# H's parts turned by TensorE instead of by DMA, spare transposes in two waits, and the last output tile stored in halves

## The chip, the core and the metric

One core of a Trainium2 chip runs the whole program as a single launch. The metric is the device time of one execution in microseconds (us). Three runs of the kernel before gave 870.17, 871.32 and 871.70 us, median 871.32.

## The reference, cut to what matters

```python
x = x + tanh(g_xattn[0]) * xattn(layernorm(x), ctx_4096, scales and zero points)
x = x + tanh(g_ffn[0]) * ffn(layernorm(x), w_gate, w_up, w_down, ri_in, ri_mid)

def ffn(x2):                       # 1024 rows, H = 1024, I = 2752, SELECT = 128
    A, g = quant_act(x2, ri_in)    # blocks of 16 in fp8, last 128 columns twice
    gate = A @ quant_w(w_gate).T * g          # int4 blocks of 16
    up = A @ quant_w(w_up).T * g
    h = silu(gate) * up
    Am, gm = quant_act(h, ri_mid)  # gm needs the maximum of |h| over ALL rows
    return Am @ quant_w(w_down).T * gm
```

`xattn` is a product of two tensors that are rounded to 8 bits. `quant_act` scales by one number from the maximum over the whole matrix, then rounds every block of 16 columns to fp8 with a scale of its own; the last 128 columns are rounded, and what is left over is rounded again.

## The kernel before, in words

The 1024 rows are eight tiles of 128 (t = 0 to 7). There are three stages. The first loads x and ctx, multiplies them, normalises and quantises (to about 200 us). The second multiplies the quantised rows by w_gate and w_up, tile by tile and 256 columns at a time, and writes h to DRAM (`multiply`, L1214 to L1220, to 615 us). The third waits for the maximum of |h| (`spread_max`, L1281), quantises h tile by tile, transposes it and multiplies it by w_down (`down`, L1270 to L1275). Every engine has its instructions in an order that is written out by hand; semaphores tie them together.

Numbers are kept to more than 16 bits by splitting each into a high and a low half in 16 bits: a block product is three matmuls (high x high, high x low, low x high). TensorE wants the column index of h on the partitions, so each tile must be turned. `H_CUTS` (L31) cuts the 22 blocks of 128 columns of each tile into parts: six for tile 0, four for tile 1, two halves for each later one. `H_PARTS` numbers them from 0. For one part the steps are:

- VectorE prepares it: `start_part` (L1753, two instructions), then `end_part` (L1762), which waits for ScalarE's `floor_magic` (L1081, L1085) and makes three sweeps (L1767, L1768, L1769). In the last part of a tile `quantise_twice` (L1447) follows for the outliers. It then signals `am_ready`.
- For the first `PE_PARTS` = 2 parts TensorE turns the part in 32 bits into a bank `tb` (`turn_h` L1264, `turn_piece` L1163, L1169), ScalarE copies the high half out (`hi_part` L876, L879) and VectorE subtracts it for the low half (`lo_part` L1408, L1411). The result lies in `amT`.
- For all others ScalarE and VectorE make the halves unturned in `nat_h` (L1104, L1785), and SP turns them by DMA: `turn_part` (L610, L615) with one transposition each for the high and the low half in tiles 0 and 1, `turn_half` (L617, L622) with one for both from tile 2 on.

VectorE's order is the loop at L1798: start of part n, then the low half of part n - 1 (`lo_h`, L1777), then the end of part n. From tile 2 on, the low half of the last part of the tile ahead comes before the start, and `finish` (L1788, L1794), which adds the product to x, stands in its place. TensorE's order is the loop at L1283:

```python
for hf in range(2):
    last = down(t % 2, hf, range(ks.start, ks.stop))
    if ks.stop == DK:
        last.then_inc(y_done, 1)
    if hf == 0 and n + 1 < PE_PARTS:
        turn_h(n + 1)
```

`hf` are the two halves of 512 output columns. ScalarE's order is: high half of part n, then `floor_magic` of part n + 1 (L1087 to L1106). SP's list is that of L630 to L650: the transpositions of tiles 0 and 1, each tile's followed by the load of the tile two on (`load_tile` L536); then for each later tile the store of an output tile (`store_out` L625, L628), a transposition, a load of x, the other transposition, a load.

Of the kernel before, what the change touches and what calls it, by code (L numbers as in the profile page):

```python
# [9 lines left out]
F16 = mybir.dt.float16  # L10
# [5 lines left out]
P = 128  # L16
# [5 lines left out]
NT = ROWS // P  # L22
# [5 lines left out]
MW = 512  # L28
DK = -(-I // P)
DH = DK // 2  # L30
H_CUTS = ((0, 3, 7, 11, 15, 19, DK), (0, 5, DH, 16, DK)) + ((0, DH, DK),) * (NT - 2)  # L31
H_PARTS = [(t, slice(a, b)) for t, cuts in enumerate(H_CUTS) for a, b in zip(cuts, cuts[1:])]
PE_PARTS = 2
HALVES = sum(1 for t, ks in H_PARTS if t < 2)
H_SMALL = 1e-20
HPAD = DK * P
# [28 lines left out]
def gated_block(nc, x, ctx_in, g_xattn, g_ffn, s1, z1, s2, z2, w_gate, w_up, w_down, ri_in, ri_mid, out):  # L65
    x_d = x.rearrange("b l h -> (b l) h").rearrange("(t p) h -> t p h", p=P)
    out_d = out.rearrange("b l h -> (b l) h").rearrange("(t p) h -> t p h", p=P)
    ctx_d = ctx_in.rearrange("b s h -> (b s) h").rearrange("(t p) h -> t p h", p=P)

    with ExitStack() as ctx:  # L70
# [3 lines left out]
        def sem(name):  # L74
            return ctx.enter_context(nc.semaphore(name))
# [25 lines left out]
        a_lo = mid[:, 4096:8192].bitcast(F16).rearrange("p (k r) -> p k r", k=KT)  # L101
        a_both = mid[:, 0:8192].bitcast(F16).rearrange("p (q r) -> p q r", q=2 * KT)
        ring = mid[:, 8192:16384].bitcast(F16).rearrange("p (s v k n) -> p s v k n", s=2, v=2, k=KT)
        amT = mid[:, 0:2 * DK * P].bitcast(F16).rearrange("p (s g v k r) -> p s g v k r", s=2, g=2, v=2, k=DH)
        o = 2 * DK * P
        mgh = mid[:, o:o + DH * P]
        o += DH * P
# [17 lines left out]
        o += 4 * H  # L125
        ro_a = big[:, o:o + 4 * SELECT].rearrange("p (s n) -> p s n", s=4)
        p_ring = big[:, 0:KT * 2 * PW].bitcast(F16).rearrange("p (v k n) -> p v k n", v=2, k=KT)
        nat_h = wbuf[:, :, :].rearrange("p b h -> p (b h)")[:, 0:HPAD].bitcast(F16).rearrange("p (g v n) -> p g v n", g=2, v=2)
        silu = sb("silu", [P, 2, UW], F32)
        h_out = sb("h_out", [P, 2, UW], F32)  # L130
        a_nat = [x[:, :, :].rearrange("p s n -> p (s n)").bitcast(BF16) for x in (silu, h_out)]
# [3 lines left out]
        ident = sb("ident", [P, P], F32)  # L135
# [156 lines left out]
        def part_of(t, k):  # L292

            return next(n for n, (at, ks) in enumerate(H_PARTS) if at == t and ks.start <= k < ks.stop)

        def parts_in(t, g):

            return [n for n, (at, ks) in enumerate(H_PARTS) if at == t and ks.start // DH == g]

        def nat_part(v, ks):  # L300

            g = ks.start // DH
            return nat_h[:, g, v, (ks.start - g * DH) * P:(ks.stop - g * DH) * P]

        def turned_part(i, v, ks):

            g = ks.start // DH
            return amT[:, i, g, v, ks.start - g * DH:ks.stop - g * DH, :]

        def loads_before(b, u):  # L310

# [6 lines left out]
        def buf(n):  # L318

            return (n + 1) % 4  # L320
# [5 lines left out]
        def _(sp):  # L326
# [283 lines left out]
            def turn_part(n):  # L610

                t, ks = H_PARTS[n]
                sp.wait_ge(nat_h_lo, n - PE_PARTS + 1)
                for v in range(2):
                    sp.dma_start_transpose(turned_part(t, v, ks), nat_part(v, ks)).then_inc(part_turned[n], 16)  # L615

            def turn_half(t, i, g):  # L617

                if g == 0:
                    sp.wait_ge(y_done, 2 * (t - 1))  # L620
                sp.wait_ge(nat_h_lo, part_of(t, g * DH) - PE_PARTS + 1)
                sp.dma_start_transpose(amT[:, i, g, :, :, :].rearrange("p v k r -> p (v k) r"),  # L622
                                       nat_h[:, g, :, :].rearrange("p v n -> p (v n)")).then_inc(h_turned[g], 16)

            def store_out(t, i):  # L625

                sp.wait_ge(y_out, t + 1)
                sp.dma_start(out_d[t], x1_t[:, i, :]).then_inc(out_stored[i], 16)  # L628

            for n in range(PE_PARTS, HALVES):  # L630
                turn_part(n)
                t, ks = H_PARTS[n]
                if ks.stop == DK:

                    sp.wait_ge(turned, PE_PARTS)
                    load_tile(t + 2, t)
            for t in range(2, NT):
                i = t % 2
                store_out(t - 2, i)
# [4 lines left out]
                turn_half(t, i, 1)  # L644
                if t + 2 < NT:
                    load_tile(t + 2, i)
            for t in (NT - 2, NT - 1):
                store_out(t, t % 2)
            for i in range(2):
                sp.wait_ge(out_stored[i], 16 * (NT // 2))  # L650
            sp.wait_ge(x1_gone, 16 * X1_FIRST)
            sp.wait_ge(x1_stored, 16 * (NT - X1_FIRST))

# [144 lines left out]
        def _(act):  # L798
# [289 lines left out]
            for n, (t, ks) in enumerate(H_PARTS):  # L1088
                if n < PE_PARTS:
                    hi_part(n, n % 4, turned_part(t, 0, ks), ks.stop - ks.start, P)  # L1090
                else:
                    if n == PE_PARTS:

                        act.wait_ge(nat_lo, UNITS_D * UNIT_PIECES + PIECE_LOOP)
                    act.wait_ge(am_ready, n + 1)
                    g = ks.start // DH
                    if t in (1, 2) and ks.start == g * DH:

                        for m in parts_in(t - 1, g):
                            if m >= PE_PARTS:  # L1100
                                act.wait_ge(part_turned[m], 32)
                    elif t > 2:
                        act.wait_ge(h_turned[g], 16 * (t - 2))
                    act.activation(nat_part(0, ks), h_in[:, t % 2, ks.start * P:ks.stop * P], ACT.Copy).then_inc(nat_h_hi, 1)  # L1104
                if n + 1 < len(H_PARTS):
                    floor_magic(n + 1, H_PARTS[n + 1][1])  # L1106
# [3 lines left out]
        def _(pe):  # L1110
            pe.wait_ge(consts_made, 2)
            def spread_max(column, out):

                return pe.transpose(out, column.to_broadcast([P, P]), ident[:])

            def turn_x(t):

# [116 lines left out]

            for n in range(P_PIECES):
                pe.wait_ge(piece_turned[buf(n)], 16)
            for m in OPENING[0:2]:
                multiply_open(m)
            for j in range(4):
# [30 lines left out]
            def down(i, hf, ks):  # L1270
                for k in ks:
                    for left, right in ((0, wd_hi), (0, wd_lo), (1, wd_hi)):
                        last = pe.matmul(acc[2 * i + hf][:], amT[:, i, k // DH, left, k % DH, :], right[:, k, hf * MW:(hf + 1) * MW],  # L1273
                                         start=(k == 0 and left == 0 and right is wd_hi), stop=(k == DK - 1 and left == 1))
                return last  # L1275


            for b in range(3):
                pe.wait_ge(piece_turned[b], turns_before(b, UNITS_D) * 16)
            pe.wait_ge(part_max, 2)  # L1280
            spread_max(gmx[:, 1:2], tb[3][:, 0:P]).then_inc(all_max, 1)  # L1281
            turn_h(0)
            for n, (t, ks) in enumerate(H_PARTS):  # L1283
                if n < PE_PARTS:

                    pe.wait_ge(lo_done, n + 1)
                elif t < 2:
                    pe.wait_ge(part_turned[n], 32)
# [14 lines left out]
        def _(dve):  # L1303
# [484 lines left out]
            def finish(t, i):  # L1788

                dve.wait_ge(x1_loaded[i], 16 * (t // 2 + 1))  # L1790
                for hf in range(2):
                    dve.wait_ge(y_done, 2 * t + (hf + 1))
                    xs = x1_t[:, i, hf * MW:(hf + 1) * MW]
                    last = dve.scalar_tensor_tensor(out=xs, in0=acc[2 * i + hf][:], scalar=gs[:, 5:6], in1=xs,  # L1794
                                                    op0=ALU.mult, op1=ALU.add)
                last.then_inc(y_out, 1)

            for n, (t, ks) in enumerate(H_PARTS):  # L1798
                i = t % 2
# [48 lines left out]
```

## Time and profile before

| what | value |
|---|---|
| median of three runs | 871.32 us |
| the profiled execution's own time | 870.89 us |
| its span in the trace | 869.0 us |
| TensorE matmul, busy | 738.5 us, 85% |
| VectorE, busy | 617.9 us, 71% |
| GpSimd, busy | 356.6 us, 41% |
| ScalarE, busy | 305.8 us, 35% |
| TensorE's share of the chain that ended last | 73% |
| VectorE's share of that chain | 19% |
| mean granted TensorE clock | 0.947 |

The span is the part of the execution that the profiler's instructions cover. The chain follows the last instruction back to what released each step. Matmuls are pipelined and their ends are modelled, so in a row with a count the time from the first start to the next start says more than a mean. A granted clock of 1.00 is 2.4 GHz and 0.50 is 1.2 GHz.

### The profile page before, as it was taken

To read this page: it belongs to the slowest core of one execution; us is meant where nothing else is said; L and a number is where in the kernel's file an instruction comes from. 1 tells how busy PE (TensorE), PEld (TensorE's weight loads), DVE (VectorE), ACT (ScalarE), POOL (GpSimd) and SP (SyncE) were. 2 spreads that over 40 slices of the span, in tenths; PEclk is the share of its full clock that TensorE was granted. 3 is DMA by queue.
4 is the path that set the end of the run, shared out by engine and by line. 5 is a ranking of instruction groups with operands and counts; after the bars stand their busy time and mean duration, and the time that the engine had idled before them with its cause. 6 is when DMAs were issued, how large, how long until landed. Compare 5 with 4: busy or idle time off the path is not lost.

```text
span 869.0 us, 10408 instructions
## 1 busy us (share of the span) xinstructions
PE 738.5 (85%) x3478; PEld 336.5 (39%) x3483; DVE 617.9 (71%) x1006; ACT 305.8 (35%) x370; POOL 356.6 (41%) x194
## 2 busy tenths in 40 slices
PE   1488300399999999999999999999698799999998
PEld 0234100154544444444444444444243344444443
DVE  5789999999265656565757676732699999989710
ACT  3657595333133434344434343520122122211100
POOL 4992789523156666666657585820000000000000
PEclk9998755599999999999999999999799999999999
DMA  8810757733449796979797979843224665663420
GB/s 315 312 50 34 209 173 190 170 64 80 75 95 210 162 220 159 222 163 232 162 220 168 228 165 220 185 104 116 98 42 118 164 158 151 174 151 101 101 58 24
DMA packets 228355, 131.36 MB, mean 151 GB/s; under 512 B 201312, under 2 KB 212576, under 8 KB 227296
## 3 DMA queue, kind: packets, MB, share of 16 engines
q1 hardware_dynamic: 228320, 130.92, 61.8%
q8 instruction: 18, 0.29, 0.1%
q14 instruction: 17, 0.14, 0.0%
HBM read 61.88 MB, written 19.66 MB: 94 GB/s over the span
## 4 chain that ended last, share of the span: by engine, by line
PE 73%; DVE 19%; POOL 4%; DMA 2%; issue 1%; ACT 1%; SPq 0%; DVEq 0%; ACTq 0%
PE acc L1218 48%; PE acc L1273 24%; POOL big L688 2%; DVE big L1484 2%; DVE tb L1393 1%; DVE big L1488 1%; PE acc L1154 1%; DVE big L1366 1%; DVE bst L1315 1%; DVE big L1468 1%; DVE tb L1473 1%; DMA mid<-wbuf 1%; DVE h_in L1417 1%; POOL mid L690 1%; DMA big<-in_x_dram 1%
## 5 line engine op out<-in xcount | busy, mean ns | idle before, releaser
L1218 PE MATMUL acc<-mid 128*128 128x512 f16 x1920 | 415.2, 379 | 0.8 <-DVE h_out L1505 0.8
L1218 PEld LDWEIGHTS acc<-mid 128*128 128x128 f16 x1920 | 187.7, 98 | 227.2 <-DVE h_out L1505 1.2
L1273 PE MATMUL acc<-big,mid 128*128 128x512 f16 x1056 | 232.1, 383 | 9.7 <-DMA mid<-wbuf 8.6
L779 POOL TENSOR_TENSOR h_in<-wbuf,h_in 128x1024 f16<-128x1024 f32 (+1 forms) x56 | 114.4, 2044 | 113.1 <-ACT h_in L1056 113.0
L1273 PEld LDWEIGHTS acc<-big,mid 128*128 128x128 f16 x1056 | 103.7, 99 | 137.5 <-issue 9.1
L696 POOL TENSOR_TENSOR wbuf<-wbuf,w_inv 128x1024 f32<-128x1024 f32 (+1 forms) x67 | 124.9, 1870 | 39.9 <-DVE w_inv L1399 39.9
L1505 DVE SCALAR_TENSOR_TENSOR h_out<-acc,gs,silu 128x256 f32<-128x256 f32 (+1 forms) x88 | 41.7, 474 | 121.7 <-ACT silu L908 95.7
L1393 DVE TENSOR_REDUCE tb<-wbuf 128x64 f32<-128x1024 f32 (+1 forms) x67 | 79.0, 1179 | 40.3 <-DMA wbuf<-in_L_ffn_w_gate_dram 21.5
L1056 ACT ACTIVATE h_in<-wbuf 128x1024 f16<-128x1024 f32 (+1 forms) x56 | 57.0, 1019 | 119.1 <-DVE wbuf L1405 119.1
L858 ACT ACTIVATE wbuf<-wbuf 128x1024 f32<-128x1024 f32 (+1 forms) x67 | 68.1, 1016 | 82.8 <-POOL wbuf L696 82.0
L1218 PE MATMUL acc<-big,mid 128*128 128x384 f16 x192 | 33.4, 336 | 48.1 <-DMA mid<-big 48.1
L908 ACT ACTIVATE silu<-acc,gs 128x256 f32<-128x256 f32 (+1 forms) x88 | 40.1, 455 | 76.2 <-PE acc L1218 73.3
L1405 DVE SCALAR_TENSOR_TENSOR wbuf<-wbuf,tb 128x1024 f32<-128x1024 f32 (+1 forms) x56 | 65.1, 1163 | 0.3 <-issue 0.2
L1104 ACT ACTIVATE wbuf<-h_in 128x1408 f16<-128x1408 f32 (+4 forms) x20 | 22.1, 1105 | 112.3 <-DVE h_in L1461 60.8
L1218 PEld LDWEIGHTS acc<-big,mid 128*128 128x128 f16 x192 | 19.2, 100 | 62.0 <-issue 50.1
L1794 DVE SCALAR_TENSOR_TENSOR mid<-acc,gs,mid 128x512 f32<-128x512 f32 x16 | 11.6, 745 | 40.9 <-PE acc L1273 40.9
L1085 ACT ACTIVATE mid<-mid,floor_bias 128x1408 f32<-128x1408 f32 (+7 forms) x22 | 24.8, 1128 | 44.4 <-DVE mid L1760 44.4
L1510 DVE TENSOR_REDUCE hm<-h_out 128x256 f32 (+2 forms) x88 | 34.0, 387 | 2.6
L714 POOL TENSOR_TENSOR big<-big 128x1024 f16<-128x1024 f32 x8 | 18.8, 2372 | 41.0 <-ACT big L903 41.0
L688 POOL TENSOR_SCALAR big<-big 128x1024 f32<-128x1024 f32 x8 | 29.5, 3684 | 11.3 <-ACT big L814 10.7
L1154 PE MATMUL acc<-mid,big 128*128 128x512 bf16 x125 | 32.7, 418 | 0.2
L1399 DVE RECIPROCAL w_inv<-tb 128x64 f32<-128x64 f32 (+1 forms) x56 | 30.2, 539 | 2.1 <-DVE tb L1396 0.2
(161 smaller groups left out, 616.4 us busy)
## 6 DMA issues: line engine op xcount, KB each, us to landing
h_in<-h_d SPq DMA_DIRECT2D x8, 1376.0 KB, 7.0
wbuf<-in_L_ffn_w_gate_dram SPq DMA_DIRECT2D x21, 512.0 KB, 4.2
wbuf<-in_L_ffn_w_up_dram SPq DMA_DIRECT2D x21, 512.0 KB, 4.1
h_d<-h_out SPq DMA_DIRECT2D x80, 128.0 KB, 3.4
big<-in_ctx_dram SPq DMA_DIRECT2D x16, 512.0 KB, 7.0
wbuf<-in_L_ffn_w_down_dram SPq DMA_DIRECT2D x16, 512.0 KB, 4.5
big<-in_x_dram SPq DMA_DIRECT2D x8, 512.0 KB, 6.7
x_d<-big SPq DMA_DIRECT2D x8, 512.0 KB, 3.0
```

The costliest lines, as they stand in the source:

```text
L688: pool.tensor_scalar(w, w, 255.0, MAGIC, ALU.min, ALU.add).then_inc(ctx_round, 1)
L696: pool.tensor_tensor(w, w, spread(w_inv[0:rows, b, 0:cols // BLK]), ALU.mult).then_inc(w_scaled, 1)
L779: pool.tensor_tensor(nat[s % 4][:, H:H + cols], wbuf[:, s % 4, 0:cols], nat[s % 4][:, 0:cols], ALU.subtract)\
L858: act.activation(wbuf[0:rows, b, 0:cols], wbuf[0:rows, b, 0:cols], ACT.Copy, bias=MAGIC, scale=W_UP)\
L908: act.activation(silu[:, m % 2, 0:cols], acc[m % 4][:, 0:cols], ACT.Silu, scale=gs[:, 2:3]).then_inc(silu_done, 1)
L1056: act.activation(nat[s % 4][:, 0:cols], wbuf[:, s % 4, 0:cols], ACT.Copy).then_inc(nat_hi, 1)
L1154: pe.matmul(acc[pair(t) + hf][:], aT[:, k, t * P:(t + 1) * P], ctxq[:, b * KT + k, hf * MW:(hf + 1) * MW], start=(k == 0), stop=False)
L1218: last = pe.matmul(acc[m % 4][:, 0:cols], left[:, k, s * P:(s + 1) * P], w[:, right, k, 0:cols], start=(k == 0 and left is a_hi and right ...
L1273: last = pe.matmul(acc[2 * i + hf][:], amT[:, i, k // DH, left, k % DH, :], right[:, k, hf * MW:(hf + 1) * MW], start=(k == 0 and left == ...
L1393: dve.tensor_reduce(top, blocks(wbuf[0:rows, b, 0:cols]), AX_X, ALU.max, apply_absolute_value=True).then_inc(scale_step, 1)
L1405: dve.scalar_tensor_tensor(out=w, in0=w, scalar=MAGIC, in1=spread(block_scale(b, looped)[0:rows, 0:cols // BLK]), op0=ALU.subtract, op1=AL ...
L1505: dve.scalar_tensor_tensor(out=h_out[:, m % 2, 0:cols], in0=acc[m % 4][:, cols:2 * cols], scalar=gs[:, 2:3], in1=silu[:, m % 2, 0:cols], o ...
```

## The change

Five edits. (1) `PE_PARTS` becomes 7: all six parts of tile 0 and the first of tile 1 are turned by TensorE. (2) Tile 1's first cut is at block 4, not 5. (3) The high and low half of a part lie side by side in `nat_h` and in `amT`, and one transposition turns both; SP loads tile 2 once TensorE has turned tile 0. (4) TensorE transposes the identity into a bank that nobody reads: 14 times (`WARM`) in the wait ahead of the gate and up products, and 6 and 22 times around the maximum of |h|. (5) The last output tile is finished and stored in two halves.

```diff
-H_CUTS = ((0, 3, 7, 11, 15, 19, DK), (0, 5, DH, 16, DK)) + ((0, DH, DK),) * (NT - 2)
+H_CUTS = ((0, 3, 7, 11, 15, 19, DK), (0, 4, DH, 16, DK)) + ((0, DH, DK),) * (NT - 2)
-PE_PARTS = 2
+PE_PARTS = 7
+WARM = 14
+FIRST_PARTS = sum(1 for t, ks in H_PARTS if t == 0)
...
+        def part_at(v, ks):
+            first = 2 * (ks.start // DH) * DH + 2 * (ks.start % DH) + v * (ks.stop - ks.start)
+            return first, first + (ks.stop - ks.start)
...
+        def nat_both(ks):
+            return nat_h[:, part_at(0, ks)[0] * P:part_at(1, ks)[1] * P]
+        def turned_both(i, ks):
+            return amT[:, i, part_at(0, ks)[0]:part_at(1, ks)[1], :]
...
                 sp.wait_ge(nat_h_lo, n - PE_PARTS + 1)
-                for v in range(2):
-                    sp.dma_start_transpose(turned_part(t, v, ks), nat_part(v, ks)).then_inc(part_turned[n], 16)
+                sp.dma_start_transpose(turned_both(t, ks), nat_both(ks)).then_inc(part_turned[n], 16)
...
+            sp.wait_ge(turned, FIRST_PARTS)
+            load_tile(2, 0)
             for n in range(PE_PARTS, HALVES):
                 turn_part(n)
-                t, ks = H_PARTS[n]
-                if ks.stop == DK:
-                    sp.wait_ge(turned, PE_PARTS)
-                    load_tile(t + 2, t)
+            sp.wait_ge(turned, PE_PARTS)
+            load_tile(3, 1)
...
-            for t in (NT - 2, NT - 1):
-                store_out(t, t % 2)
+            store_out(NT - 2, 0)
+            for hf in range(2):
+                sp.wait_ge(y_out, NT + hf)
+                sp.dma_start(out_d[NT - 1][:, hf * MW:(hf + 1) * MW], x1_t[:, 1, hf * MW:(hf + 1) * MW]).then_inc(out_half[hf], 16)
...
+            def keep_busy(n, bank):
+                for _ in range(n):
+                    pe.transpose(tb[bank][:, 0:P], ident[:], ident[:])
...
             for n in range(P_PIECES):
                 pe.wait_ge(piece_turned[buf(n)], 16)
+            pe.wait_ge(nat_a_lo, 1)
+            for i in range(WARM):
+                pe.transpose(acc[3][:, 0:P], ident[:], ident[:])
...
+            keep_busy(6, 2)
             pe.wait_ge(part_max, 2)
             spread_max(gmx[:, 1:2], tb[3][:, 0:P]).then_inc(all_max, 1)
+            keep_busy(22, 2)
             turn_h(0)
...
-                last.then_inc(y_out, 1)
+                    if hf == 1 or t == NT - 1:
+                        last.then_inc(y_out, 1)
```

Three places of the instruction order, before and after. First TensorE's list from the maximum of |h| on, before (`gmx` is the maximum, `tb` the bank a transpose writes, `acc` the product):

```order
L1114 MATMUL tb<-ident,gmx 128x128
L1169 MATMUL tb<-ident,h_in 128x128 x3
L1273 MATMUL acc<-big,mid 128x512 x9
L1169 MATMUL tb<-ident,h_in 128x128 x4
L1273 MATMUL acc<-big,mid 128x512 x1047
```

and in the changed kernel:

```order
L1137 MATMUL tb<-ident 128x128 x6
L1132 MATMUL tb<-ident,gmx 128x128
L1137 MATMUL tb<-ident 128x128 x22
L1192 MATMUL tb<-ident,h_in 128x128 x3
L1300 MATMUL acc<-big,mid 128x512 x9
L1192 MATMUL tb<-ident,h_in 128x128 x4
L1300 MATMUL acc<-big,mid 128x512 x21
L1192 MATMUL tb<-ident,h_in 128x128 x4
L1300 MATMUL acc<-big,mid 128x512 x24
L1192 MATMUL tb<-ident,h_in 128x128 x4
L1300 MATMUL acc<-big,mid 128x512 x24
```

The transposes of part m + 1 now stand between the two output halves of part m up to part 6; 28 spare ones stand around the maximum. Second, ScalarE's list for parts 1 to 3 (L1085 is `floor_magic`), before:

```order
L879 ACTIVATE mid<-tb 128x512
L1085 ACTIVATE mid<-mid,floor_bias 128x512
L1104 ACTIVATE wbuf<-h_in 128x512
L1085 ACTIVATE mid<-mid,floor_bias 128x512
L1104 ACTIVATE wbuf<-h_in 128x512
L1085 ACTIVATE mid<-mid,floor_bias 128x512
```

and in the changed kernel (L897 is the copy out of `tb`, L1103 `floor_magic`):

```order
L897 ACTIVATE mid<-tb 128x512
L1103 ACTIVATE mid<-mid,floor_bias 128x512
L897 ACTIVATE mid<-tb 128x512
L1103 ACTIVATE mid<-mid,floor_bias 128x512
L897 ACTIVATE mid<-tb 128x512
L1103 ACTIVATE mid<-mid,floor_bias 128x512
```

The high halves of parts 2 to 6 are now copied out of the bank that TensorE writes, not out of `h_in`; the places in the list are the same. Third, SP's list in tiles 0 and 1, before:

```order
L615 DMA_TRANSPOSE mid<-wbuf 128x4x128 x6
L615 DMA_TRANSPOSE mid<-wbuf 128x3x128 x2
L537 ISA
L537 DMA h_in<-h_d 128x2752
L615 DMA_TRANSPOSE mid<-wbuf 128x5x128 x2
L615 DMA_TRANSPOSE mid<-wbuf 128x6x128 x2
L615 DMA_TRANSPOSE mid<-wbuf 128x5x128 x2
L615 DMA_TRANSPOSE mid<-wbuf 128x6x128 x2
```

and in the changed kernel:

```order
L553 DMA h_in<-h_d 128x2752
L630 DMA_TRANSPOSE mid<-wbuf 128x14x128
L630 DMA_TRANSPOSE mid<-wbuf 128x10x128
L630 DMA_TRANSPOSE mid<-wbuf 128x12x128
L553 ISA
L553 DMA h_in<-h_d 128x2752
```

Sixteen transpositions became three, of 14, 10 and 12 blocks, and the load of tile 2 comes before them.

## Rows read from the trace of the kernel before

**Rows 1.** The page, its groups of instructions: the gate and up products.
```profile
L1218 PE MATMUL acc<-mid 128*128 128x512 f16 x1920 | 415.2, 379 | 0.8 <-DVE h_out L1505 0.8
```

**Rows 2.** The chain that ended last: start (us), length, engine, work.
```profile
200.55 414.65 PE acc L1218 x1944
...
659.19 27.87 PE acc L1273 x129
687.07 5.15 DMA mid<-wbuf
692.35 172.80 PE acc L1273 x792
```

**Rows 3.** Timeline of the opening: start, length, engine, line, work, idle time before.
```profile
160.12 4.20 POOL L714 TENSOR_TENSOR big<-big 128x1024 f16<-128x1024 f32 x2
...
166.91 9.54 PE L1218 MATMUL acc<-big,mid 128*128 128x384 f16 x48 [48.06 <-DMA mid<-big]
```

**Rows 4.** Timeline of the start of the down product, and the first matmuls of tile 2.
```profile
622.15 0.90 PE L1169 MATMUL tb<-ident,h_in 128*128 128x128 f32 x3 [4.79 <-DVE h_in L1769]
...
624.23 3.74 PE L1273 MATMUL acc<-big,mid 128*128 128x512 f16 x9 [1.18 <-DVE mid L1411]
...
627.80 0.60 PE L1169 MATMUL tb<-ident,h_in 128*128 128x128 f32 x4
...
628.24 7.29 PE L1273 MATMUL acc<-big,mid 128*128 128x512 f16 x33
628.44 0.60 ACT L879 ACTIVATE mid<-tb 128x512 f16<-128x512 f32 x1 [4.25 <-PE tb L1169]
...
629.07 0.69 DVE L1411 TENSOR_TENSOR mid<-tb,mid 128x512 f16<-128x512 f32 x1 [1.58 <-ACT mid L879]
...
659.19 2.98 PE L1273 MATMUL acc<-big,mid 128*128 128x512 f16 x13 [2.26 <-DMA mid<-wbuf]
...
692.35 19.98 PE L1273 MATMUL acc<-big,mid 128*128 128x512 f16 x84 [4.49 <-DMA mid<-wbuf]
```

**Rows 5.** Timeline of VectorE in tile 0: sweeps of parts 3 to 5, outlier steps.
```profile
635.18 0.69 DVE L1769 TENSOR_TENSOR h_in<-h_in,mid 128x512 f32<-128x512 f32 x1
...
639.24 0.69 DVE L1769 TENSOR_TENSOR h_in<-h_in,mid 128x512 f32<-128x512 f32 x1
...
641.70 0.49 DVE L1767 SCALAR_TENSOR_TENSOR h_in<-mid,h_in 128x320 f32<-128x320 f32 x1
...
646.40 0.29 DVE L1461 TENSOR_TENSOR h_in<-h_in,ro_h 128x128 f32<-128x128 f32 x1
```

**Rows 6.** VectorE's low part in tile 1; landing of SP's transpositions of L622.
```profile
653.58 0.82 DVE L1785 TENSOR_TENSOR wbuf<-h_in,wbuf 128x640 f16<-128x640 f32 x1
...
DMA to landing us min/median/max: 5.1/5.2/6.9
```

**Rows 7.** Windows and a burst: PE, PEld, DVE, ACT, POOL busy; granted clock; DMA; GB/s.
```profile
71.00:71.50 0.50, 0.13 (x2) 0.14 (x3) 0.50 (x5) 0.46 (x1) 0.00 (x0) 0.67 0.00 0
...
77.50:78.00 0.50, 0.50 (x3) 0.18 (x2) 0.47 (x1) 0.50 (x1) 0.00 (x0) 0.50 0.00 0
...
73.30 1.04 PE L1122 MATMUL tb<-identb,h_out 128*128 128x128 bf16 x8 [0.90 <-DVE h_out L1359]
...
617.00:617.50 0.50, 0.29 (x1) 0.13 (x1) 0.29 (x2) 0.00 (x0) 0.00 (x0) 0.80 0.56 197
...
657.00:658.00 1.00, 0.00 (x0) 0.00 (x0) 1.00 (x2) 0.35 (x1) 0.00 (x0) 1.00 1.17 215
...
692.00:692.50 0.50, 0.15 (x1) 0.13 (x2) 0.43 (x3) 0.00 (x0) 0.00 (x0) 0.90 0.64 229
...
695.50:696.00 0.50, 0.50 (x3) 0.17 (x2) 0.50 (x1) 0.50 (x1) 0.00 (x0) 0.69 0.00 0
```

**Rows 8.** The end: SP's last store, and the window in which its bytes move.
```profile
865.95 0.34 SPq L628 DMA_DIRECT2D out_dram<-mid  x1
...
867.00:868.00 1.00, 0.00 (x0) 0.00 (x0) 0.00 (x0) 0.00 (x0) 0.00 (x0) 1.00 1.01 410
```

More of the change, by code:

```diff
@@ L103, in gated_block @@
         ring = mid[:, 8192:16384].bitcast(F16).rearrange("p (s v k n) -> p s v k n", s=2, v=2, k=KT)
-        amT = mid[:, 0:2 * DK * P].bitcast(F16).rearrange("p (s g v k r) -> p s g v k r", s=2, g=2, v=2, k=DH)
+        amT = mid[:, 0:2 * DK * P].bitcast(F16).rearrange("p (s k r) -> p s k r", s=2, r=P)
         o = 2 * DK * P
@@ L127, in gated_block @@
         p_ring = big[:, 0:KT * 2 * PW].bitcast(F16).rearrange("p (v k n) -> p v k n", v=2, k=KT)
-        nat_h = wbuf[:, :, :].rearrange("p b h -> p (b h)")[:, 0:HPAD].bitcast(F16).rearrange("p (g v n) -> p g v n", g=2, v=2)
+        nat_h = wbuf[:, :, :].rearrange("p b h -> p (b h)")[:, 0:HPAD].bitcast(F16)
         silu = sb("silu", [P, 2, UW], F32)
@@ L260, in gated_block @@
         y_out = sem("y_out")
+        out_half = [sem(f"out_half{i}") for i in range(2)]
         out_stored = [sem(f"out_stored{i}") for i in range(2)]
@@ L298, in parts_in @@
             return [n for n, (at, ks) in enumerate(H_PARTS) if at == t and ks.start // DH == g]
+        def part_at(v, ks):
+            first = 2 * (ks.start // DH) * DH + 2 * (ks.start % DH) + v * (ks.stop - ks.start)
+            return first, first + (ks.stop - ks.start)
         def nat_part(v, ks):
-            g = ks.start // DH
-            return nat_h[:, g, v, (ks.start - g * DH) * P:(ks.stop - g * DH) * P]
+            a, b = part_at(v, ks)
+            return nat_h[:, a * P:b * P]
         def turned_part(i, v, ks):
-            g = ks.start // DH
-            return amT[:, i, g, v, ks.start - g * DH:ks.stop - g * DH, :]
+            a, b = part_at(v, ks)
+            return amT[:, i, a:b, :]
+        def nat_both(ks):
+            return nat_h[:, part_at(0, ks)[0] * P:part_at(1, ks)[1] * P]
+        def turned_both(i, ks):
+            return amT[:, i, part_at(0, ks)[0]:part_at(1, ks)[1], :]
         def loads_before(b, u):
@@ L621, in turn_half @@
                 sp.wait_ge(nat_h_lo, part_of(t, g * DH) - PE_PARTS + 1)
-                sp.dma_start_transpose(amT[:, i, g, :, :, :].rearrange("p v k r -> p (v k) r"),
-                                       nat_h[:, g, :, :].rearrange("p v n -> p (v n)")).then_inc(h_turned[g], 16)
+                ks = H_PARTS[part_of(t, g * DH)][1]
+                sp.dma_start_transpose(turned_both(i, ks), nat_both(ks)).then_inc(h_turned[g], 16)
             def store_out(t, i):
@@ L646, in _ @@
                     load_tile(t + 2, i)
-            for t in (NT - 2, NT - 1):
-                store_out(t, t % 2)
+            store_out(NT - 2, 0)
+            for hf in range(2):
+                sp.wait_ge(y_out, NT + hf)
+                sp.dma_start(out_d[NT - 1][:, hf * MW:(hf + 1) * MW], x1_t[:, 1, hf * MW:(hf + 1) * MW]).then_inc(out_half[hf], 16)
             for i in range(2):
-                sp.wait_ge(out_stored[i], 16 * (NT // 2))
+                sp.wait_ge(out_stored[i], 16 * (NT // 2 - i))
+                sp.wait_ge(out_half[i], 16)
             sp.wait_ge(x1_gone, 16 * X1_FIRST)
@@ L1100, in _ @@
                             if m >= PE_PARTS:
-                                act.wait_ge(part_turned[m], 32)
+                                act.wait_ge(part_turned[m], 16)
                     elif t > 2:
@@ L1270, in down @@
             def down(i, hf, ks):
+                hi, lo = (turned_part(i, v, ks) for v in range(2))
                 for k in ks:
-                    for left, right in ((0, wd_hi), (0, wd_lo), (1, wd_hi)):
-                        last = pe.matmul(acc[2 * i + hf][:], amT[:, i, k // DH, left, k % DH, :], right[:, k, hf * MW:(hf + 1) * MW],
-                                         start=(k == 0 and left == 0 and right is wd_hi), stop=(k == DK - 1 and left == 1))
+                    for left, right in ((hi, wd_hi), (hi, wd_lo), (lo, wd_hi)):
+                        last = pe.matmul(acc[2 * i + hf][:], left[:, k - ks.start, :], right[:, k, hf * MW:(hf + 1) * MW],
+                                         start=(k == 0 and left is hi and right is wd_hi), stop=(k == DK - 1 and left is lo))
                 return last
@@ L1287, in _ @@
                 elif t < 2:
-                    pe.wait_ge(part_turned[n], 32)
+                    pe.wait_ge(part_turned[n], 16)
                 else:
```

## The prediction

> **What bounds the kernel now.** I read the page first, then the chain that ended last, then the stretches around the two places where TensorE stands idle, and last the granted clock in short windows. The page's group of the gate and up products shows 1920 matmuls with only 0.8 us of idle time ahead of them, and that wait is for VectorE (h_out, L1505) [rows 1]. In the chain, TensorE takes over at 200.55 us and runs without a wait to 615.20. The second stage (the down product) begins behind that: 129 matmuls from 659.19 to 687.06, a transposition that is issued at 687.07, and 792 matmuls from 692.35 to 865.15 [rows 2]. So before 200 us and between 615 and 692 us VectorE and the transpositions decide; elsewhere TensorE does, at 27.87 / 129 = 0.216 us for a matmul. What the change is worth is what it does to the moment 692.35, to the speed just behind it, and to the last store.
>
> **The opening (14 transposes of the identity).** TensorE waits there until 166.91 us; the first of the two rows of POOL's residual work is half over at 162.2, which is what releases the new transposes [rows 3]. At half clock one costs 0.21 us (three take 0.90 us with their latency, and at full clock four start and end within 0.44 us before the next matmul begins, 0.11 each [rows 4]), so 14 end near 165.2, 1.7 us before they could delay anything. If they bring the clock up, the first ten or so matmuls (384 columns, 0.32 us in place of 0.16) give back 1.7 us. I cost this at **nothing**: VectorE releases TensorE at 200.55 [rows 1, 2], and its own work ahead of that does not wait for TensorE. The 0.8 us wait grows to 2.5 us. If that cover were gone, the gain would be 1.7 us at most.
>
> **Tile 0 of H by TensorE.** Four more parts of tile 0 and the first part of tile 1 (four blocks, was five by DMA) now go as the first two did: TensorE turns part m+1 between the two output halves of part m, ScalarE copies the high part out of PSUM, VectorE makes the low part. I follow three clocks. TensorE for a part of four blocks: 12 matmuls (2.59), four transposes (0.44), 12 matmuls (2.59), together **5.62 us**. VectorE's own work for one: the ends of its last sweep lie 4.05 us apart now (635.18 to 639.24) [rows 5]. But VectorE makes the low part m+1 *before* it may do the three sweeps of part m+2, and that low part now needs the transposes, which stand behind 12 matmuls. From the start of part m on TensorE it is 2.59 + 0.60 (transposes to their last end) + 0.04 + 0.61 (ScalarE) + 0.03 + 0.69 (VectorE) [rows 4] = 4.56 us until the low part m+1 is made. So TensorE is always fed and VectorE is held to TensorE's pace of 5.62 us, not its own 4.05.
>
> With the clock up: part 0 is ready at 622.10; its three transposes, 0.90 us now [rows 4], take 0.5, so the first matmul is at 623.85, 0.4 earlier; 9 matmuls to 625.8; part 1 is ready at 626.0, its transposes take 626.05 to 626.49, the second half ends at 628.43. There part 1 starts; part 3 starts two cycles on, at 628.43 + 2 x 5.62 = 639.67, and the low part 4 is made at 639.67 + 4.56 = 644.23. The sweeps of part 5, which now begin at 641.70, thus begin at 644.26: **2.6 us late**; the outlier steps behind them [rows 5] move to 645.8 to 649.2. In tile 1 TensorE must finish 12 + 9 matmuls between the transposes of part 5 (649.25) and those of part 6 (654.11), and ScalarE's step for the seven-block part comes behind that copy, some 0.2 us more for VectorE; the low part of seven blocks in place of six adds 0.1 to 0.2. From there on VectorE's list is the old one. The transposition of tile 2's first half is issued at 687.07 + 2.9 and lands as long after it as now (5.3 us [rows 2]): **695.25 instead of 692.35, +2.9 us**. Bounds: +2.0 (nothing added in tile 1, 0.5 saved in handing over) and +4.3, below.
>
> **Tile 1's own wait.** TensorE is through part 6 (24 matmuls) at 661.7. The seven-block part is swept at 660.1, its low part is made at 662.6, and one transposition of 14 blocks must land. The nearest rows: two of five blocks landed 4.8 us after the low part (653.58 + 0.82 to 659.19), 22 blocks take 5.2 [rows 4, 6]. I take 4.4, so 667.0: an idle time of 5.3 us where the old one was 2.3. Behind it 108 matmuls, 23.3 us, and 1.7 for eight of them at half clock, end at 692.0. That is before 695.25, so this wait costs nothing by itself; it is the cover of the single transposition and of the new cut too, which I cost at nothing. SP passes fewer transpositions (3 in place of 16) ahead of the third tile's load; the load of tile 2 moves up to about 649.7, off the path either way.
>
> **The clock behind 692.** In the trace the clock fell during idle times of 4.5 us (692.0 to 692.5), and of about 2 us (617.0 to 617.5 and 71.0 to 71.5), and stayed up across 2.3 us (657 to 658) [rows 7]. The new idle time ahead of tile 2 is 3.3 us. It lies between, and I take it to fall (three chances in four): the restart then loses about what it loses now: the clock is at half from 692.4 to 695.65 (0.90 and 0.69 of full speed in the two windows of half a microsecond [rows 7]), and 3.3 us at half clock are 1.65 us lost. I put down -0.2 for a shorter slow piece; ends 0 and -1.7.
>
> **The 28 transposes at 615 us** cost nothing in place: six take 0.64 us (1.3 at half clock) behind 615.2 and the maximum is wanted at 617.07; 22 take 2.4 us, or 4.7 at half clock, and end at 622.05 at the latest, before part 0 is ready.
>
> **The last tile in halves.** The last store is issued at 865.95; its 512 KB move at 410 GB/s [rows 8], 1.3 us. Half of it is **-0.6 us**; ends 0 and -0.9. The first half goes 7 us earlier, beside nothing.
>
> **Sum** against this execution's own 870.89 us (span 869.0): +2.9 - 0.2 - 0.6 = +2.1, 873.0. The median of the three runs, 871.32, is 0.43 above it, so **873.4** on its scale. About 0.2% (1.7 us) is what a measurement of this kernel can tell from no change.
>
> **Rivals.**
> *Cold start.* The spare transposes do not bring the clock up, or it is low again when the down product begins, since from 622.1 (at full clock from 619.7) to 623.85 TensorE does nothing but the three transposes of part 0. Evidence: it stood at half at 77.5 although 16 transposes and then matmuls had run from 71.4 on [rows 7]. Then nine matmuls take 3.7 us as now [rows 4], the transposes of part 1 come at 627.5, and everything behind them 1.4 us later: the low part 4 at 645.6, tile 2's half at 696.6 (+4.25), sum +4.25 - 0.4 - 0.6 = +3.2, **874.5**. By "TensorE: Matmul & The Clock Gate" of the Trainium skill, Part 4, the full clock does not engage for transposes, which would make this the certain case; the burst at 71 to 74 us agrees with it but had gaps, so the trace leaves it open.
> *Clock kept ahead of tile 2.* If the 3.3 us do not let it fall, the restart is 1.5 us quicker than in my sum: **871.9**. For it: 2.3 us kept it [rows 7].
> *Faster, the other sign: the hand-over does not pace VectorE.* This is so only if the low part m+1 is made before VectorE has finished preparing part m+2, that is within 4.05 us of the last one; I find 5.62. If it held, VectorE would lose none of the 2.6 us and save the 1.6 us for which it now stands idle ahead of its second low part (627.5 to 629.07 [rows 4]): 692.35 - 1.6 + 0.3, full clock behind it (-1.7), -0.6 for the store: 867.3, **867.7**. Against it stands the order of TensorE's list: the transposes are behind 12 matmuls.
>
> **How the numbers follow.** My forecast (clock up at 623.8, down at 695) 0.38; cold start 0.30; clock kept 0.14; not paced 0.10; other mishaps, of either sign, 0.08. Slower than 873.06: 0.65 of the forecast (0.25), nine tenths of the cold start (0.27), and 0.04 of the rest: 0.56. Faster than 869.58: the last rival and a few hundredths of the rest, 0.11. Within: 0.33. The range of 8 in 10 leaves out the unpaced case and the far end of the cold one: 870.9 to 875.3.
>
> **What would show it.** In the new trace: a wait of about 1 to 1.7 us of VectorE ahead of each low part of parts 2 to 4, released by ScalarE's copy out of tb; TensorE without a gap from 626 to 648; then an idle time near 5 us in tile 1 and near 3 us before tile 2, released by transpositions; the first matmul of tile 2 at 695.3 (696.6 if cold); TensorE's wait at 200 us grown to about 2.5. I am wrong if VectorE does not wait in tile 0, or if the moment of 692.35 does not move back.

## The result, and the profile after

| | before | changed |
|---|---|---|
| median | 870.75 us (4 runs) | 876.34 us (4 runs, 875.49 to 876.90) |
| ratio | 1 | 1.006, interval 1.004 to 1.008 |
| the profiled execution's own time | 870.89 us | 875.49 us |
| its span | 869.0 us | 873.5 us |

The change makes the kernel slower by 0.6%. The direction was forecast, the size was not: 873.4 was the forecast, 875.3 the upper end of the range.

The page's groups of the changed kernel, where L1241 is the gate and up product and L1300 the down product:

```profile
L1241 PE MATMUL acc<-mid 128*128 128x512 f16 x1920 | 415.2, 379 | 0.4 <-DVE h_out L1534 0.4
...
L1300 PE MATMUL acc<-big,mid 128*128 128x512 f16 x1056 | 235.8, 386 | 8.4 <-DMA mid<-wbuf 7.2
```

TensorE's wait for VectorE in the opening went from 0.8 us [rows 1] to 0.4. The waits of the down product for transpositions sum to 7.2 us, where the page of the kernel before has 8.6. So TensorE's idle time in these groups fell, and what is lost does not stand in this view.

The chain that ended last (start, length, engine, work), to be laid beside [rows 2]:

```profile
200.55 414.65 PE acc L1241 x1944
...
623.86 4.02 PE acc L1300 x9
...
664.93 4.35 DMA mid<-wbuf
669.32 22.73 PE acc L1300 x95
692.05 5.13 DMA mid<-wbuf
697.32 172.80 PE acc L1300 x792
870.15 0.75 DVE mid L1823
```

The long chain of gate and up products begins at 200.55 and lasts 414.65 us in both kernels, to the hundredth. So nothing ahead of 615.20 moved. The first matmul of tile 2 was at 692.35 and is at 697.32: **+4.97 us**. The 792 matmuls behind it take 172.80 us in both. From the end of VectorE's last instruction (870.90) to the end of the span it is 2.6 us, where it was 3.1. So +4.97 - 0.5 is the whole difference of the two spans, 4.5 us.

The timeline of tile 0 in the changed kernel, TensorE's transposes (L1192) and VectorE's low parts (L1440), which answers to [rows 4, 5]:

```profile
622.14 0.55 PE L1192 MATMUL tb<-ident,h_in 128*128 128x128 f32 x3 [2.44 <-DVE h_in L1798]
...
627.67 1.06 PE L1192 MATMUL tb<-ident,h_in 128*128 128x128 f32 x4
...
629.40 0.69 DVE L1440 TENSOR_TENSOR mid<-tb,mid 128x512 f16<-128x512 f32 x1 [2.14 <-ACT mid L897]
...
633.56 0.60 PE L1192 MATMUL tb<-ident,h_in 128*128 128x128 f32 x4
...
634.83 0.69 DVE L1440 TENSOR_TENSOR mid<-tb,mid 128x512 f16<-128x512 f32 x1 [1.55 <-ACT mid L897]
...
639.18 0.60 PE L1192 MATMUL tb<-ident,h_in 128*128 128x128 f32 x4
...
640.45 0.69 DVE L1440 TENSOR_TENSOR mid<-tb,mid 128x512 f16<-128x512 f32 x1 [1.74 <-ACT mid L897]
...
644.80 0.60 PE L1192 MATMUL tb<-ident,h_in 128*128 128x128 f32 x4
...
646.06 0.69 DVE L1440 TENSOR_TENSOR mid<-tb,mid 128x512 f16<-128x512 f32 x1 [1.72 <-ACT mid L897]
646.67 0.48 DVE L1796 SCALAR_TENSOR_TENSOR h_in<-mid,h_in 128x320 f32<-128x320 f32 x1
```

The sets of transposes are 5.6 to 5.9 us apart, and ahead of the low parts of parts 1 to 4 VectorE stands idle for 1.55 to 2.14 us until ScalarE's copy is there. The sweeps of part 5 begin at 646.67; they began at 641.70 [rows 5]. That is 4.97 us, the whole delay, and it is there before tile 1 begins.

Windows of the changed kernel (busy PE, PEld, DVE, ACT, POOL; granted clock; DMA; GB/s), beside [rows 7]:

```profile
164.00:165.00 1.00, 1.00 (x7) 1.00 (x6) 0.96 (x2) 0.00 (x0) 0.34 (x1) 0.50 1.15 212
165.00:165.50 0.50, 0.50 (x3) 0.21 (x1) 0.50 (x2) 0.00 (x0) 0.00 (x0) 0.67 1.15 214
165.50:166.00 0.50, 0.03 (x1) 0.00 (x0) 0.47 (x2) 0.00 (x0) 0.00 (x0) 1.00 1.09 184
...
622.50:623.00 0.50, 0.19 (x2) 0.00 (x0) 0.47 (x2) 0.28 (x1) 0.00 (x0) 0.71 0.00 0
...
629.00:629.50 0.50, 0.50 (x3) 0.23 (x2) 0.10 (x1) 0.50 (x2) 0.00 (x0) 0.50 0.00 0
629.50:630.00 0.50, 0.50 (x4) 0.23 (x3) 0.50 (x1) 0.48 (x1) 0.00 (x0) 0.96 0.00 0
...
697.00:698.00 1.00, 0.68 (x3) 0.32 (x4) 0.83 (x4) 0.00 (x0) 0.00 (x0) 0.90 0.66 242
698.00:699.00 1.00, 1.00 (x4) 0.33 (x3) 0.90 (x4) 0.00 (x0) 0.00 (x0) 0.50 0.59 234
```

The clock came up at 165.3 behind nothing but spare transposes, stayed up to 622.7, fell there and rose at 629.5. It was at half (1.2 GHz) for the nine matmuls of part 0's first output half, for the four transposes of part 1 and for the first two or so of the 21 matmuls behind them. It fell again in tile 1's wait, at 667.1, and, last, at 697.8, after the restart.

### The profile page after: what moved, and what is told of

The parts are those of the page before. It is cut to its first block, busy times and chain, and to the rows that moved or that the text cites. A ratio compares the mean times of both kernels' runs of the same rounds, so it can differ in the third digit from the quotient of the medians.

```text
span 873.5 us, 10523 instructions
## 1 busy us (share of the span) xinstructions
PE 745.4 (85%) x3544; PEld 343.9 (39%) x3544; DVE 618.2 (71%) x1006; ACT 305.8 (35%) x370; POOL 356.4 (41%) x194
## 4 chain that ended last, share of the span: by engine, by line
PE 74%; DVE 16%; POOL 3%; DMA 3%; ACT 1%; SPq 1%; issue 1%; DVEq 0%; ACTq 0%
PE acc L1241 47%; PE acc L1300 25%; DVE big L1513 2%; POOL big L706 2%; DVE big L1517 2%; PE acc L1177 1%; DVE tb L1422 1%; DMA mid<-wbuf 1%; DMA big<-in_ctx_dram 1%; DVE big L1497 1%; DVE big L1395 1%; DVE tb L1502 1%; DVE bst L1344 1%; POOL mid L708 1%; DMA wbuf<-in_L_ffn_w_gate_dram 1%
## 5 line engine op out<-in xcount | busy, mean ns | idle before, releaser
L1241 PE MATMUL acc<-mid 128*128 128x512 f16 x1920 | 415.2, 379 | 0.4 <-DVE h_out L1534 0.4
L1241 PEld LDWEIGHTS acc<-mid 128*128 128x128 f16 x1920 | 187.8, 98 | 226.7 <-DVE h_out L1534 0.9
L1300 PE MATMUL acc<-big,mid 128*128 128x512 f16 x1056 | 235.8, 386 | 8.4 <-DMA mid<-wbuf 7.2
L1300 PEld LDWEIGHTS acc<-big,mid 128*128 128x128 f16 x1056 | 104.7, 99 | 136.6 <-issue 10.4
L1122 ACT ACTIVATE wbuf<-h_in 128x1408 f16<-128x1408 f32 (+3 forms) x15 | 19.1, 1270 | 98.4 <-DVE h_in L1490 55.8
L1262 PE MATMUL acc<-ident 128*128 128x128 f32 x14 | 3.1, 417 | 45.4 <-POOL big L732 45.4
L1103 ACT ACTIVATE mid<-mid,floor_bias 128x1408 f32<-128x1408 f32 (+7 forms) x22 | 24.8, 1128 | 41.5 <-DVE mid L1789 41.5
L1241 PE MATMUL acc<-big,mid 128*128 128x384 f16 x192 | 32.0, 326 | 3.2 <-DMA mid<-big 3.2
L1177 PE MATMUL acc<-mid,big 128*128 128x512 bf16 x128 | 30.6, 395 | 0.0
```

The source lines that it names most:

```text
L1177: pe.matmul(acc[pair(t) + hf][:], aT[:, k, t * P:(t + 1) * P], ctxq[:, b * KT + k, hf * MW:(hf + 1) * MW], start=(k == 0), stop=False)
L1241: last = pe.matmul(acc[m % 4][:, 0:cols], left[:, k, s * P:(s + 1) * P], w[:, right, k, 0:cols], start=(k == 0 and left is a_hi and right ...
L1300: last = pe.matmul(acc[2 * i + hf][:], left[:, k - ks.start, :], right[:, k, hf * MW:(hf + 1) * MW], start=(k == 0 and left is hi and righ ...
```

## Experiments

All are edits of the changed kernel. Instruction lists that are identical over the gate and up products reached the end of the gate and up products between 614.1 and 617.1 us in the profiles of these kernels, so that single times scatter by some 3 us. I therefore read the third stage against its own start: E is the end of the long chain of gate and up products, R the first matmul of tile 2. "VectorE's wait" is its idle time ahead of the low parts, for ScalarE's copy out of `tb`, between 612 and 712 us. For the kernel before and for the changed one its lines are:

```profile
DVE mid L1411 <- ACT mid L879: 2.0, 2, 1.6
...
DVE mid L1440 <- ACT mid L897: 7.2, 4, 2.1
```

| kernel | VectorE's wait | R - E | 792 matmuls | ratio to before (interval) |
|---|---|---|---|---|
| before | 2.0 | 77.15 | 172.80 | 1 |
| changed | 7.2 | 82.12 | 172.80 | 1.006 (1.004 to 1.008) |
| e1_parts_back | 2.2 | 77.58 | 173.47 | 1.0006 (0.9992 to 1.0021) |
| e2_no_spare | 7.4 | 82.22 | 172.80 | 1.0052 (1.0034 to 1.007) |
| e3_clock_kept | 4.8 | 79.78 | 171.11 | 1.0012 (0.9996 to 1.0028) |
| e4_whole_store | 7.2 | 82.08 | 172.80 | 1.0055 (1.0034 to 1.0076) |
| e5_short_tile0 | 2.2 | 77.15 | 171.12 | 0.9978 (0.9965 to 0.999) |
| e6_two_kept | 0.3 | 75.64 | 172.69 | 0.9968 (0.9953 to 0.9984) |
| e7_no_warm | 7.3 | 82.06 | 172.80 | 1.0058 (1.0036 to 1.008) |
| e8_three_kept | 1.3 | 76.53 | 171.11 | 0.9966 (0.9947 to 0.9985) |
| e10_turn_ahead | 4.5 | 79.27 | 172.79 | 1.0022 (1.0006 to 1.0038) |
| e11_two_busy | 0.3 | 76.47 | 170.95 | 0.996 (0.9945 to 0.9975) |

R - E less VectorE's wait is 74.8 to 75.4 us in all of them but e11 (76.2), where spare transposes reach into the restart. So R - E follows VectorE's wait. The column of the 792 matmuls is a term of its own, the clock behind the restart: at 171.1 us it stayed up, at 172.8 us it was low for some 3 us.

### The parts back

```diff
-H_CUTS = (..., (0, 4, DH, 16, DK))    PE_PARTS = 7
+H_CUTS = (..., (0, 5, DH, 16, DK))    PE_PARTS = 2
```

SP's list is as before, with one transposition for each part.

> The changed kernel with the parts as before: two of them turned by TensorE, tile 1's first cut at block 5, SP's list in the old order; one transposition for both halves, the spare transposes and the last tile in halves stay. Pacing theory (VectorE is held to TensorE's pace in tile 0, and that is all of the loss): the sweeps of part 5 begin at about 641.7 us as before, the first matmul of tile 2 at 692.4, no wait of VectorE ahead of the low parts 2 to 5; with the store's 0.5 us the median is 870.2, 6 us under the changed kernel. Rival (the spare transposes cost, or the joined transpositions land late): at least 873, with the moment of 692.4 at 694 or later.

The wait of VectorE ahead of its low parts in this kernel (total, times, longest; E is 617.13):

```profile
DVE mid L1439 <- ACT mid L896: 2.2, 1, 2.2
```

Its chain:

```profile
202.48 414.65 PE acc L1240 x1944
...
694.71 173.47 PE acc L1299 x792
```

R - E is 77.58, 4.5 us less than in the changed kernel, and there is one wait, not four. The joined transpositions, the spare transposes and the halves, all still there, cost no more than 0.4 us together at this point. By the absolute marks this looks like the rival, whose price was 694 or later: R is at 694.71 and not at 692.4. But the long chain began 1.93 us late (202.48 in place of 200.55), ahead of everything that was edited, and only 0.4 us is left of the rest. The median was 872.58 beside 871.89 for the kernel before, not 1 us under it; the 0.5 us of the store did not show in the times. The parts, with the new cut and the order of SP's list that go with them, are the cause.

### The clock kept up

```diff
-            keep_busy(22, 2)
+            keep_busy(40, 2)
             turn_h(0)
+            keep_busy(10, 2)
```

> The changed kernel with 40 spare transposes in place of 22 behind the maximum and 10 more behind the transposes of part 0, so that TensorE idles for less than a microsecond before the first down matmul. Theory (the clock's fall at 622.7 is one term, the pacing the other): the clock stays up from 615 to 660, part 0's nine matmuls take 1.95 us and not 4.0, the sweeps of part 5 begin at 644.3 in place of 646.7, tile 2 starts 2.4 us earlier, near 694.9, and the time falls by 2.4 (by 0.7 to 1 if the clock is then found low for longer behind 695), to about 874. Rival (all of the loss is the clock): the time falls to 871 or less.

VectorE's wait in this kernel:

```profile
DVE mid L1441 <- ACT mid L897: 4.8, 4, 1.7
```

The chain of the same kernel:

```profile
199.43 414.65 PE acc L1241 x1944
...
693.86 171.11 PE acc L1300 x792
```

R - E is 693.86 - 614.08 = 79.78: the clock's share of the 4.97 us is 2.34, the pace's share is 2.63. The forecast case of the prediction gave +2.9 for the pace with the clock up. "All of the loss is the clock" falls. A part of the better time is a third thing: TensorE stood idle for 1.90 us ahead of tile 2, the clock stayed up, and the 792 matmuls took 171.11 us in place of 172.80.

### TensorE made faster than VectorE in tile 0

```diff
-            def down(i, hf, ks):
+            def down(i, hf, ks, short=False):
...
+                        if short and right is wd_lo:
+                            continue
...
-                    last = down(t % 2, hf, range(ks.start, ks.stop))
+                    last = down(t % 2, hf, range(ks.start, ks.stop), t == 0)
```

This leaves out w_down's low half in tile 0, 44 matmuls.

> The changed kernel without the high x low products of tile 0 (it leaves out 44 of the 132 matmuls of that tile, that is w_down's low half there). TensorE's cycle for a four-block part is then 16 x 0.216 + 0.44 = 3.9 us, less than VectorE's 4.05. Pacing theory: VectorE no longer waits ahead of the low parts 3 to 5, its sweeps of part 5 begin at 641 and not at 646.7, tile 2 starts at 691.5 to 692, and the time is about 870, though TensorE's own saving in tile 0 (9.5 us) comes before a wait for VectorE anyway. Rival (TensorE's work, not its pace over VectorE, is what counts): all 9.5 us are saved, 866.8. Rival (the loss comes from tile 1's new wait for its 14-block transposition): no change in where tile 2 starts, 697.

VectorE's wait in this kernel:

```profile
DVE mid L1442 <- ACT mid L897: 2.2, 4, 0.9
```

Its chain:

```profile
635.78 0.66 PE tb L1192 x4
...
639.91 0.67 PE tb L1192 x4
...
692.49 171.12 PE acc L1302 x792
```

TensorE's sets of transposes are now 4.13 us apart (635.78 to 639.91), close to VectorE's own 4.05, and VectorE's last two waits are 0.25 and 0.23 us. R - E is 77.15, the value of the kernel before to the hundredth, although seven parts still go by TensorE, the clock is still low at the start (from 623.2 to 630.0) and the new wait in tile 1 is still there (5.25 us). This settles that VectorE is held to TensorE's pace, and that tile 1's wait costs nothing. Of the 9.5 us of matmuls left out 5.0 came back at R.

### Two parts, then three, with the clock kept

```diff
-PE_PARTS = 7
+PE_PARTS = 2        (3 in e8_three_kept)
```

Both with the old cuts, with SP's list in the old order and with the spare transposes of e3_clock_kept.

> Two parts by TensorE and the old cuts, one transposition for both halves, the last tile in halves, and enough spare transposes (6, 40 and 10) that the clock stays up until the first down matmul. From the end of the gate and up products, theory: part 0's matmuls end 2 us earlier, VectorE's wait ahead of its second low part goes from 1.6 us to about 0.6, so the first matmul of tile 2 comes 490.3 us after the start of the long gate and up chain (491.8 before, 496.8 in the changed kernel, 494.4 with seven parts and the clock kept); with the store in halves the whole is 1.5 to 2 us under the kernel before. Rival (the spare transposes buy nothing without the parts): 491.8 and no more than 0.5 us under the kernel before.

VectorE's wait in this kernel:

```profile
DVE mid L1440 <- ACT mid L896: 0.3, 1, 0.3
```

Its chain:

```profile
168.94 448.16 PE acc L1240 x2112
...
692.74 172.69 PE acc L1299 x792
```

E is 168.94 + 448.16 = 617.10, R - E is 75.64, which puts R 490.3 us behind the start of the long chain (taken as E - 414.65), as forecast: 1.5 us less than before.

> As e6_two_kept, but with three parts by TensorE. If each part that TensorE turns beyond the second holds VectorE by the difference of the two paces, this one costs 0.8 us (the first such wait is shorter, since VectorE is then not yet ahead): the first matmul of tile 2 at 491.1 us after the start of the long chain. If the loss in the changed kernel comes from the seventh part and the new cut in tile 1 alone, it equals e6_two_kept.

VectorE's wait in this kernel:

```profile
DVE mid L1440 <- ACT mid L896: 1.3, 2, 1.1
```

Its chain:

```profile
200.19 414.65 PE acc L1240 x1944
...
691.37 171.11 PE acc L1299 x792
```

R - E is 76.53: the third part costs 0.89 us (forecast 0.8), and VectorE's wait grew by 1.0 us. One more part, one more wait; tile 1, which has the old cuts and goes by DMA in both kernels, has no share in it.

The restart, 171.11 in place of 172.69, does not speak for three parts. In e8_three_kept the clock fell in tile 1's wait, so that tile 1's 132 matmuls took 30.35 us, where they took 28.66 in e6_two_kept. That filled the wait ahead of tile 2 (2.71 us in place of 4.47), and there the clock then stayed up. What was lost in tile 1 was hidden under VectorE's work, and what was kept at the restart counted.

### The transposes ahead of both halves

This is an edit of e3_clock_kept.

```diff
+                if 0 < n < PE_PARTS - 1:
+                    turn_h(n + 1)
                 for hf in range(2):
...
-                    if hf == 0 and n + 1 < PE_PARTS:
+                    if hf == 0 and n == 0:
                         turn_h(n + 1)
```

> e3_clock_kept (seven parts, clock kept) with the transposes of part m+1 ahead of both output halves of part m for m = 1 to 5, not between them. If only the pace counts (one set of transposes for each 5.62 us of TensorE), VectorE gains 0.8 us once and tile 2 starts 79.0 us after the end of the gate and up products (79.8 in e3_clock_kept, 77.2 before). If it is the place behind 12 matmuls that costs, VectorE's waits in tile 0 go away and tile 2 starts at 76 to 77.

VectorE's wait in this kernel:

```profile
DVE mid L1443 <- ACT mid L897: 4.5, 5, 1.7
```

Its chain:

```profile
200.74 414.65 PE acc L1241 x1944
...
694.66 172.79 PE acc L1300 x792
```

R - E is 694.66 - 615.39 = 79.27, only 0.5 us under e3_clock_kept (79.0 was expected if only the pace counts). The place behind 12 matmuls is worth half a microsecond; that there is one set of transposes for each 5.6 us of TensorE is worth the rest.

### Spare transposes, one place at a time

Without the 28 around the maximum of |h|:

> The changed kernel without the 28 spare transposes around the maximum of |h| (the 14 ahead of the gate and up products stay). If they had an effect, the clock falls at 617 as before, the three transposes of part 0 take 0.9 us in place of 0.55 and the first down matmul starts at 624.2 in place of 623.86; it may be up again by 627.5. Theory: within 0.7 us of the changed kernel either way, since the clock was low for the first nine matmuls in both. Rival (spare transposes cost time in place): 1 us or more faster than the changed kernel.

R - E is 82.22 against 82.12, the median 876.94. Its chain:

```profile
202.27 414.65 PE acc L1241 x1944
...
699.14 172.80 PE acc L1300 x792
```

They bought nothing in the changed kernel. Without them the clock fell at 620.8, 3.9 us behind E, and not at 617.3 (2.1 us behind E) as in the kernel before; with them it fell at 622.7, 7.5 us behind E. All three are ahead of the nine matmuls of part 0, nearly all of which were slow in each of the three kernels.

Without the 14 in the opening:

> The changed kernel without the 14 spare transposes ahead of the gate and up products. Theory: no difference in time (within 0.7 us of the changed kernel's 876.3, ratio to the kernel before 1.005 to 1.007); the clock rises at 170.2 as before and not at 165.2, and the first product takes 5.8 us in place of 4.1, while VectorE still releases TensorE at 200.5. Rival (they delay something in the opening): 1 us or more faster.

Its chain:

```profile
200.59 414.65 PE acc L1241 x1944
...
697.30 172.80 PE acc L1300 x792
```

No difference: 876.49 beside 876.34, and the long chain starts at 200.59. The clock rose at 171.7 there, later than the expected 170.2, and even that did not count. The timeline of the opening of the changed kernel shows where the faster product went:

```profile
162.39 3.14 PE L1262 MATMUL acc<-ident 128*128 128x128 f32 x14 [45.38 <-POOL big L732]
166.93 4.07 PE L1241 MATMUL acc<-big,mid 128*128 128x384 f16 x24 [1.40 <-DMA mid<-big]
172.77 4.07 PE L1241 MATMUL acc<-big,mid 128*128 128x384 f16 x24 [1.76 <-DMA mid<-big]
...
200.55 5.35 PE L1241 MATMUL acc<-mid 128*128 128x512 f16 x24 [0.37 <-DVE h_out L1534]
```

The first product takes 4.07 us, and the second then waits 1.76 us for the next transposition. The products behind these two start at 176.68, where they started at 176.29 in the kernel before. What the clock gave was taken by a DMA 6 us later, and VectorE released TensorE at 200.55 either way.

With 32 more ahead of tile 2, on e6_two_kept:

> e6_two_kept with 32 more spare transposes (3.4 us) at the start of TensorE's wait ahead of tile 2. Theory: the clock is then not low at the restart, the 792 matmuls of tiles 2 to 7 take 171.1 us in place of 172.7, the restart itself does not move (75.6 us behind the end of the gate and up products), and the time is 1.6 us under e6_two_kept: ratio to the kernel before about 0.995. Rival (transposes do not keep the clock): 172.7 as well.

Its chain, with the spare transposes in it (L1136):

```profile
658.11 30.35 PE acc L1299 x132
688.46 3.49 PE tb L1136 x32
691.96 170.95 PE acc L1299 x792
```

The 792 matmuls take 170.95 us and not 172.69, as expected, but the restart moved, against the expectation: R - E is 76.47, was 75.64. The clock had fallen in tile 1's wait, as in e8_three_kept, so tile 1's matmuls ended 1.8 us later behind E than in e6_two_kept, and the 32 began and ended later by as much, some 0.8 us after the tile had landed. Had tile 1 run as in e6_two_kept, they would have ended before it. The ratio of 0.996 cannot be told from e6_two_kept's 0.9968.

### The store whole

> The changed kernel with the last output tile finished and stored whole. Theory: 0.5 us slower than the changed kernel; from the end of the last VectorE instruction to the end of the span 3.1 us in place of 2.6. Rival: the halves gain nothing, 2.6 us as well.

The last instruction of VectorE in this kernel:

```profile
870.16 0.75 DVE mid L1820
```

VectorE ends at 870.91 and the span at 874.1, 3.2 us later, against 2.6 in halves. The 0.6 us of the forecast is there in the profiles; the medians (876.27 and 876.34) do not show it.

## Why the prediction was wrong

- **The opening costs nothing**: right, though for another reason than cover at the end: the wait at 200 us did not grow to 2.5 us but fell to 0.37, since the gain was lost to a transposition at 172.77.
- **VectorE is held to TensorE's pace in tile 0**: right. Forecast 5.62 us for each part and waits of 1 to 1.7 us; measured 5.62 (633.56 to 639.18) and 1.55 to 1.74, and 2.14 for the one at half clock. With the clock kept, the step's +2.9 us measured +2.63.
- **The clock at the start is the step that failed.** I took the clock to be up when part 0 was ready, so that its nine matmuls would end at 625.8, as likelier (0.38) than the cold start (0.30). They ended at 627.9. The cold start came, and was dearer than I had priced it: I gave it the old 3.7 us for nine matmuls and a clock that is up again by 627.5. In fact the clock fell *later* than before, at 622.7, and was low until 629.5, over nine matmuls, four transposes and the first of those behind them: 4.02 and 0.85 us, and a wait of 2.14 us. The cold rival's +4.25 us measured +4.97; e3_clock_kept puts the clock's share of it at 2.34 us. Of that +4.97 tile 1 added nothing: the sweeps of part 5 are late by 4.97 and so is tile 2, where I had put down 0.3 us for tile 1.
- **The range** ended short of the cold start as it came: the cold rival's 874.5 lies inside it, and 0.7 us more for the cold start, 0.4 us more for the restart (that rival took 0.4 off) and some 0.3 us for the store, the profiled difference and rounding carry it to 875.9, past 875.3.
- **The restart ahead of tile 2**: I took off 0.2 us for a shorter slow piece. It is 172.80 us in both, so nothing. The idle time was 2.27 us, not 3.3: tile 1's matmuls began 2.3 us later than forecast, at 669.32, and ran at half clock until 673.9, some 0.6 us more lost than I had put down. That the clock is low for the first of the 792 matmuls came true, in part by luck: it fell 0.5 us after the restart, and two other kernels here kept it across longer idle times, 2.71 and 2.98 us.
- **The store**: forecast -0.6; 0.5 between the two spans, 0.6 against e4_whole_store. Right.
- Against the kernel's own execution the terms now give +4.97 + 0 - 0.5 = +4.5, and the profiled executions differ by 4.6 us. The rest up to the 5.6 us of the medians is taken for scatter of four runs each, which is not shown: the median of the kernel before is 870.75 with a fourth run of 869.10, where the forecast stood on 871.32, and the three kernels of the table that differ from the changed one by at most 0.1 us in R - E had ratios of 1.0052 to 1.0058.
- The faster rival is refuted by the waits. The cold rival's name for its cause, that transposes do not engage the full clock, is refuted too, for 32-bit transposes of the identity: they raised the clock at 165.3 and held it to 622.7, and with 40 and 10 of them it did not fall ahead of part 0 at all (e3_clock_kept). "TensorE: Matmul & The Clock Gate" of the Trainium skill, Part 4, says beside a measured 16-bit transpose that the full clock does not engage for transpose mode. The 16-bit transposes of these traces, the burst of [rows 7], leave it open; for the 32-bit ones of this kernel the measurement decides.

The versions with two or three parts by TensorE and the clock kept up beat both kernels, by 0.3% over the kernel before (their intervals lie below 1) and by 0.9% over the changed one, the last from the two ratios and not from runs side by side.

## What to carry to other kernels

When work moves from a DMA queue to an engine that takes its instructions in order and is nearly full, add up the *cycle* of every hand-over, not the latency of one: an engine that had run ahead at 4.05 us is held to the 5.62 us of the engine that it now waits for, each time round, and a later stage pays the sum. Read the price at the next fixed point behind it, here the first matmul of tile 2, and not in the idle time of the busy engine, which fell here. Spare work that holds the clock is worth something only if it reaches up to the first instruction that counts: fill the wait to its end, but not beyond.

## What the runs showed of the hardware that was not expected

- 32-bit transposes of the identity alone raised TensorE's clock (at 165.3, 2.9 us after they began) and kept it up from 615 us to the first down product in e3, e6, e8, e10 and e11.
- Whether the clock falls does not go by the length of one idle time: ahead of tile 2 it was lost with 2.27 and 2.76 us of idle time (changed, e10_turn_ahead) and kept with 2.98 and 2.71 (e5_short_tile0, e8_three_kept). In the changed kernel it fell 0.5 us *after* work had begun again. With the same TensorE instructions behind E it fell 2.1 us behind E in the kernel before and 3.9 us behind it in e2_no_spare.
- One transposition of 14 blocks landed 4.35 us after its issue, of 22 blocks 5.1 to 5.2. The estimate of 4.4 us from the low part to the first matmul of tile 1 held (664.90 to 669.32).
- The start of the third stage moved by 3 us between profiled executions with the same instructions up to it. The cause lies ahead of the long chain, in the first 200 us, and stays open.
